# LayerNorm over partitions: variance and reciprocal root as whole-half tiles instead of compact token columns

## The chip, the cores and the metric

One core of one Trainium2 chip runs the kernel. The metric is the device time of one execution in microseconds (us): 6545.41 us is the median of three runs of the kernel before (6545.12 to 6548.72). Engines are called PE (TensorE matmul), PEld (TensorE's weight load), DVE (VectorE), ACT (ScalarE), POOL (GpSimd) and SP (the queue that issues the DMAs here).

## The reference, cut to what matters

The state x holds 16 batches of 56 tokens with 128 features each, all in fp32. Eight blocks follow one another, each adding its result to x: a six-layer diffusion transformer block with a context of 1500 tokens, a mixture of experts, a cross-attention block, an expert-choice layer, a latent cross-attention, a sparse mixer, slot attention and three fast-feed-forward trees. Every block starts from a LayerNorm of x, and the blocks have norms of their own. What matters is the norm:

```python
def _layernorm(x, axis=-1, eps=1e-05):
    m = jnp.mean(x, axis=axis, keepdims=True)
    v = jnp.var(x, axis=axis, keepdims=True)
    return (x - m) / jnp.sqrt(v + eps)

x = x + block(_layernorm(x, axis=-1), ...)     # eight times
```

In some uses the normed values are also scaled and shifted, by one factor per batch and feature (the adaptive norms of the cross-attention block) or one factor per feature.

## The kernel before, in words

x is kept in SBUF with the features on the 128 partitions and the 896 tokens (batch by batch) along the free axis. Most work is done by halves of 448 tokens, c = 0 and c = 1; `half(a, c)` is such a half. So a mean over features is a sum over partitions, and PE makes it: a matmul with `mean_w`, a 128x128 tile that holds 1/128 everywhere, leaves the mean of each token on all 128 partitions. An fp32 matmul shows as two MATMUL and two LDWEIGHTS records in the trace.

The program has one instruction stream per engine, written out by hand in `program`, block by block, and the engines meet only at semaphores. Twelve norms treat all 896 tokens at once through the helpers `ln_tensor`, `ln_scalar` and `ln_vector` (L253 to L303): the entry norm of each of the eight blocks (`LN_IN0`, `LN_MOE`, `LN_IN1`, `LN_EC`, `LN_IN2`, `LN_SM`, `LN_IN3`, `LN_FFF`), the three adaptive norms of the cross-attention block (`LN_L1(0)` to `LN_L1(2)`, with `per_batch`), and the norm of the latents (`LN_LAT`, with `per_feature`; `LN_IN3` also has `per_feature`). The norms inside the six layers of the first block (L1648, L1653, L1834 to L1839, L1987 to L1991) and those of the slot units (L3195 to L3200, L3264, L3371) have code of their own and are not touched. The first of these already takes its variance and its root over a whole half: L1653, L1991 (128x448), and the reciprocal L1839 over a quarter (128x224).

The steps of one such norm before the change, each done for c = 0 and then for c = 1:

1. PE L257: mean of the half, broadcast on all partitions, into PSUM bank c.
2. DVE L285: deviation = source minus mean.
3. ACT L274: square of the deviation into `ln_square`.
4. PE L261: four matmuls that use 112 tokens of the squares each as weights and one column of `mean_w` as the moving side; the variance of the 448 tokens comes out as a compact tile of 112 partitions by 4 columns in bank 2 + c. Both halves are 16 MATMUL records.
5. ACT L277: root of variance plus eps on the 112x4 tile, into `ln_token_stats`. Its function table is loaded ahead of it where ACT did something else before (ACT_TABLE_LOAD).
6. DVE L288: reciprocal of the 112x4 tile.
7. PE L266: four matmuls that spread the 112x4 tile to 128 partitions by 448 tokens, with a broadcast column as weights and the identity as the moving side, into bank 2 + c. Both halves are 16 MATMUL records.
8. DVE L292: deviation times the spread reciprocal root, read from PSUM, into the destination. With `per_batch` two more 128x448 operations per half follow (L297, L299), with `per_feature` one (L302); a drain stands ahead of each.

After the last half `ln_done` is signalled. PE waits for `ln_done(n, 1)`, the second half, at once behind `ln_tensor` (for instance L578, L730, L2575, L2580), except in the slot block, where a few small folding matmuls and one transposition of context tiles stand between the two (L3222 to L3225). After that wait come the router matmul L356 (expert blocks), the folding of weights L2367 (cross-attention block), the mean L257 of the following norm (`LN_LAT` behind `LN_IN2`) and the like. ACT and DVE go on in their own order: ACT to what the block does next, often with a table load, DVE to the block's own work, which mostly waits for PE.

Of the kernel before, what the change touches and what calls it, by code (L numbers as in the profile page):

```python
# [7 lines left out]
ALU, ACT, AX = mybir.AluOpType, mybir.ActivationFunctionType, mybir.AxisListType  # L8
# [4 lines left out]
HALF = T // 2  # L13
ROW, NQ = 112, 4
# [32 lines left out]
WHOLE = lambda n: n - 18 if n > LN_SLOT else n  # L47
N_WHOLE = WHOLE(N_LN)


class Signal:
# [3 lines left out]
    def __init__(self, sem, dims, step=1, base=0):  # L55
        self.sem, self.dims, self.step, self.base = sem, dims, step, base
# [44 lines left out]
def half(a, c):  # L101
    return a[:, c * HALF:(c + 1) * HALF]
# [6 lines left out]
def by_batch(a):  # L109
    return a.rearrange("p (b s) -> p b s", s=S)  # L110


def spread(cols, n):
    p, m = cols.shape
    return cols.unsqueeze(2).broadcast_to([p, m, n])


class Kernel:


    def __init__(self, nc, ctx, dr, out):
        self.nc, self.ctx, self.dr, self.out = nc, ctx, dr, out
        self.names, self.sems = {}, {}
        sb = lambda *a: self.sb(ctx, *a)
        self.x = sb("x_state", [128, T])[:, :]
        self.z = sb("block_state", [128, T])[:, :]
        self.xn = sb("x_normed", [128, T])[:, :]
        self.dev = sb("ln_deviation", [128, T])[:, :]
        self.sq = sb("ln_square", [128, T])[:, :]
        self.stats = sb("ln_token_stats", [ROW, 4, NQ])  # L130
        self.ident = sb("ident", [128, 128])
        self.ident_b = sb("ident_bf16", [128, 128], BF16)
        self.mean_w = sb("mean_weights", [128, 128])[:, :]
        self.gb = sb("adaln_scale_shift", [128, NORMS, 2, B])
        self.cond = sb("cond", [128, B])[:, :]
        self.c_mean = sb("context_mean", [KN, B, KT])
        self.c_rstd = sb("context_rstd", [KN, B, KT])
        self.eps_col = sb("eps", [128, 1])[:, :]
        self.psum = ctx.enter_context(nc.psum_tensor("psum", [128, 8, BANK], F32))
        self.consts_ready = self.events("consts_ready")  # L140
        self.in_arrived = self.events("in_arrived", step=32)
        self.ln_mean = self.events("ln_mean", N_LN, 2)
        self.ln_dev = self.events("ln_dev", N_LN, 2)
        self.ln_square = self.events("ln_square_ready", N_LN, 2)
        self.ln_var = self.events("ln_var", N_WHOLE, 2)
        self.ln_std = self.events("ln_std", N_WHOLE, 2)
        self.ln_rstd = self.events("ln_rstd", N_WHOLE, 2)
        self.ln_spread = self.events("ln_spread", N_WHOLE, 2)
        self.ln_done = self.events("ln_done", N_LN, 2)
        self.x_done = self.events("x_done", 8, 2)  # L150
        self.tokens_scored = self.events("tokens_scored", 4)
        self.rows_turned = self.events("rows_turned", 8, 2)
        self.rows_copied = self.events("rows_copied", 8, 2)
        self.gate_select = sb("gate_select", [128, 8], BF16)[:, :]
        self.gate_select32 = sb("gate_select_f32", [24, 8])[:, :]
        self.select_arrived = self.events("gate_select_arrived", step=16)
        self.select_ready = self.events("gate_select_ready")

    def sb(self, stack, name, shape, dt=F32):
        self.names[name] = self.names.get(name, 0) + 1  # L160
        if self.names[name] > 1:
            name = f"{name}_{self.names[name]}"
        return stack.enter_context(self.nc.sbuf_tensor(name, shape, dt))
# [89 lines left out]
def ln_tensor(e, k, n, src):  # L253


    for c in range(2):
        e.matmul(k.psum[:, c, 0:HALF], k.mean_w, half(src, c)).then_inc(k.ln_mean.sem, 1)  # L257
    for c in range(2):
        e.wait_ge(k.ln_square.sem, k.ln_square(n, c))
        for i in range(NQ):  # L260
            mm = e.matmul(k.psum[0:ROW, 2 + c, i:i + 1], half(k.sq, c)[:, i * ROW:(i + 1) * ROW], k.mean_w[:, 0:1])  # L261
        mm.then_inc(k.ln_var.sem, 1)
    for c in range(2):
        e.wait_ge(k.ln_rstd.sem, k.ln_rstd(WHOLE(n), c))
        for i in range(NQ):
            mm = e.matmul(k.psum[:, 2 + c, i * ROW:(i + 1) * ROW],  # L266
                          k.stats[:, 2 + c, i:i + 1].broadcast_to([ROW, 128]), k.ident[0:ROW, 0:ROW])
        mm.then_inc(k.ln_spread.sem, 1)


def ln_scalar(e, k, n):
    for c in range(2):
        e.wait_ge(k.ln_dev.sem, k.ln_dev(n, c))
        e.activation(half(k.sq, c), half(k.dev, c), ACT.Square).then_inc(k.ln_square.sem, 1)  # L274
    for c in range(2):
        e.wait_ge(k.ln_var.sem, k.ln_var(WHOLE(n), c))
        e.activation(k.stats[:, c, :], k.psum[0:ROW, 2 + c, 0:NQ], ACT.Sqrt, bias=k.eps_col[0:ROW, :]).then_inc(  # L277
            k.ln_std.sem, 1)


def ln_vector(e, k, n, src, dst, per_batch=None, per_feature=None):

    for c in range(2):
        e.wait_ge(k.ln_mean.sem, k.ln_mean(n, c))
        e.tensor_tensor(half(k.dev, c), half(src, c), k.psum[:, c, 0:HALF], ALU.subtract).then_inc(k.ln_dev.sem, 1)  # L285
    for c in range(2):
        e.wait_ge(k.ln_std.sem, k.ln_std(WHOLE(n), c))
        e.reciprocal(k.stats[:, 2 + c, :], k.stats[:, c, :]).then_inc(k.ln_rstd.sem, 1)  # L288
    for c in range(2):
        v = half(dst, c)  # L290
        e.wait_ge(k.ln_spread.sem, k.ln_spread(WHOLE(n), c))
        op = e.tensor_tensor(v, half(k.dev, c), k.psum[:, 2 + c, 0:HALF], ALU.mult)  # L292
        if per_batch is not None:
            v = by_batch(v)
            g, b = (spread(a[:, c * BH:(c + 1) * BH], S) for a in per_batch)
            e.drain()
            e.tensor_tensor(v, v, g, ALU.mult)  # L297
            e.drain()
            op = e.tensor_tensor(v, v, b, ALU.add)  # L299
        if per_feature is not None:  # L300
            e.drain()
            op = e.tensor_scalar(v, v, per_feature[0], per_feature[1], ALU.mult, ALU.add)  # L302
        op.then_inc(k.ln_done.sem, 1)  # L303
# [212 lines left out]
class GroupedExperts:  # L516
# [56 lines left out]
    def tensor(self, e):  # L573
        k = self.k
        e.wait_ge(k.x_done.sem, k.x_done(self.stage - 1, 1))
        ln_tensor(e, k, LN_MOE, k.x)
        e.wait_ge(self.router_arrived.sem, self.router_arrived())
        e.wait_ge(k.ln_done.sem, k.ln_done(LN_MOE, 1))  # L578
        tokens_tensor(e, k, 0, self.rw, self.E)
        e.wait_ge(self.chosen.sem, self.chosen())  # L580
        parts = self.parts[:, :, :, :].rearrange("p t j e -> p t (j e)")
        part_rows_tensor(e, k, 0, parts[:, :, 0:128], (0, 1), k.rows_turned)
        part_rows_tensor(e, k, 1, parts[:, :, 128:192], (2, 3), k.rows_turned)
        e.wait_ge(self.weights_arrived.sem, self.weights_arrived())
        e.wait_ge(k.rows_copied.sem, k.rows_copied(1, 1))
        e.wait_ge(self.cleared.sem, self.cleared())
        e.wait_ge(self.wide_ready.sem, self.wide_ready(1))
        self.experts.tensor(e)
# [90 lines left out]
class ExpertChoice:  # L679
# [67 lines left out]
    def scalar(self, e, ahead):  # L747
        ln_scalar(e, self.k, LN_EC)
        e.wait_ge(self.shifted.sem, self.shifted())
        e.activation(self.probs, self.probs, ACT.Exp).then_inc(self.exped.sem, 1)  # L750
        ahead.fold_scalar(e)
        self.experts.scalar(e)
# [51 lines left out]
class SparseMixer:  # L804
# [43 lines left out]
    def tensor(self, e):  # L848
        k = self.k
        e.wait_ge(k.x_done.sem, k.x_done(self.stage - 1, 1))  # L850
        ln_tensor(e, k, LN_SM, k.x)
        e.wait_ge(self.router_arrived.sem, self.router_arrived())
        e.wait_ge(k.ln_done.sem, k.ln_done(LN_SM, 1))
        tokens_tensor(e, k, 2, self.wg, self.E)
        e.wait_ge(self.gates_ready.sem, self.gates_ready())
        part_rows_tensor(e, k, 4, self.parts[:, :, :, :].rearrange("p t j e -> p t (j e)"), (0, 1), k.rows_turned)
        e.wait_ge(self.weights_arrived.sem, self.weights_arrived())
        e.wait_ge(k.rows_copied.sem, k.rows_copied(4, 1))
        e.wait_ge(k.select_ready.sem, k.select_ready())
        self.experts.tensor(e)  # L860
# [2788 lines left out]
```

## Time and profile before

| | us |
|---|---|
| median of the runs (lowest to highest) | 6545.41 (6545.12 to 6548.72) |
| the profiled execution's own time | 6548.03 |
| span of the profiled execution | 6546.2 |
| busy: PE, PEld | 6049.3, 4418.7 |
| busy: DVE, ACT, POOL | 3926.4, 3331.9, 2250.2 |

The span is the time between the first and the last record of the profile; the execution's own time is 1.8 us longer. Busy is the sum over an engine's instructions; the PE's matmul ends are modelled. The mean granted TensorE clock is 0.95 of full speed over the whole span; around the boundaries between blocks it is lower. The twelve norms lie at 35, 3468, 3635, 3660, 3828, 4668, 4703, 4817, 4824, 5824, 6000 and 6401 us from the start of the span.

### The profile page before, as it was taken

How to read it: one execution, taken by the hardware profiler on the slowest of the kernel's cores; microseconds unless marked ns; L12 is line 12 of the kernel's file. 1: busy time of each engine (PE TensorE's matmuls, PEld its weight loads, DVE VectorE, ACT ScalarE, POOL GpSimd, SP SyncE). 2: the span in 40 equal slices, each digit the busy share in tenths (PEclk: the TensorE clock that was granted, in tenths of full speed). 3: DMA queues.
4: the chain of work that ended last, by engine and by line, in shares of the span. 5: the costliest groups of instructions: out<-in, count | busy, mean ns of one | idle time of the engine just before them, and what ended most of it. 6: DMA issues, size and time to landing. Idle time of an engine off the chain costs nothing.

```text
span 6546.2 us, 141322 instructions
## 1 busy us (share of the span) xinstructions
PE 6049.3 (92%) x56229; PEld 4418.7 (68%) x56229; DVE 3926.4 (60%) x8713; ACT 3331.9 (51%) x6403; POOL 2250.2 (34%) x2198
## 2 busy tenths in 40 slices
PE   6899999999999999999997999999879999989997
PEld 4566666666666666666664777777657777765984
DVE  3776777777777777777775344444544444444553
ACT  1565656666566665666664334444333333333664
POOL 4555555555555555555540000000011111127440
PEclk7999999999999999999998899999889999998998
DMA  1665656656566665665661000000100000021000
GB/s 55 105 108 82 102 94 103 101 92 106 86 103 101 97 102 91 102 98 96 109 90 41 18 29 29 34 33 30 26 11 15 15 10 15 15 72 47 2 1 23
DMA packets 396488, 407.90 MB, mean 62 GB/s; under 512 B 125575, under 2 KB 372946, under 8 KB 393786
## 3 DMA queue, kind: packets, MB, share of 16 engines
q1 hardware_dynamic: 395834, 398.85, 34.3%
q8 instruction: 450, 7.37, 0.6%
q14 instruction: 204, 1.67, 0.1%
HBM read 158.00 MB, written 0.46 MB: 24 GB/s over the span
## 4 chain that ended last, share of the span: by engine, by line
PE 69%; DVE 8%; POOL 7%; issue 6%; ACT 4%; DMA 2%; SPq 1%; POOLq 1%; DVEq 0%; ACTq 0%
PE psum L2244 10%; PE psum L2211 9%; PE psum L1581 6%; PE psum L1569 6%; PE psum L1555 6%; PE psum L1595 4%; PE psum L2256 4%; PE psum L1603 4%; PE psum L1701 3%; POOL slot_context L3444 2%; DVE row_max L1920 2%; PE psum L421 2%; PE psum L435 2%; PE psum L1710 1%; DMA key_stack<-key_parts 1%
## 5 line engine op out<-in xcount | busy, mean ns | idle before, releaser
L1920 DVE TENSOR_REDUCE row_max<-psum 112x1 f32<-112x500 f32 x2304 | 1443.3, 669 | 283.3 <-PE psum L1569 278.6
L2041 ACT ACTIVATE weights<-psum 125x448 f32<-125x448 f32 x2304 | 1155.3, 544 | 771.7 <-PE psum L1555 757.1
L1555 PEld LDWEIGHTS psum<-query_stack,key_stack 121*125 121x125 bf16 x9216 | 830.8, 140 | 369.5 <-issue 166.9
L1569 PE MATMUL psum<-key_stack,query_stack 97*112 97x500 bf16 x2304 | 904.8, 393 | 105.6 <-DVE row_max L1920 78.9
L1555 PE MATMUL psum<-query_stack,key_stack 121*125 121x112 bf16 x9216 | 932.7, 224 | 70.2 <-ACT weights L2041 65.0
L2244 PE MATMUL psum<-l_ctx_v,l_turned 125*128 125x128 f32 x5376 | 713.6, 281 | 16.1 <-ACT l_turned L2282 12.0
L2324 DVE TENSOR_REDUCE l_stat<-psum 128x1 f32<-128x1500 f32 (+1 forms) x224 | 391.7, 1749 | 542.3 <-PE psum L2211 542.3
L2244 PEld LDWEIGHTS psum<-l_ctx_v,l_turned 125*128 125x128 f32 x5376 | 643.1, 191 | 58.9 <-ACT l_turned L2282 40.0
L1581 PE MATMUL psum<-weights,values 125*17 125x112 f32 x18432 | 678.7, 266 | 0.2 <-ACT weights L2041 0.2
L1581 PEld LDWEIGHTS psum<-weights,values 125*17 125x17 f32 x18432 | 379.7, 98 | 264.1 <-ACT weights L2041 144.1
L2061 POOL TENSOR_TENSOR key_temp<-key_temp,rope_sin 128x500 f32<-128x500 f32 x288 | 359.5, 1248 | 502.2 <-DVE key_temp L1805 502.2
L2071 POOL TENSOR_TENSOR key_parts<-key_temp,key_parts 128x500 bf16<-128x500 f32 x288 | 327.1, 1136 | 545.1 <-ACT key_parts L1950 545.1
L2282 ACT ACTIVATE l_turned<-psum 125x512 f32<-125x512 f32 x448 | 251.3, 597 | 431.9 <-PE psum L2256 429.2
L2068 POOL TENSOR_TENSOR key_temp<-key_temp,key_parts 128x500 f32<-128x500 f32 x288 | 327.1, 1136 | 363.9 <-ACT key_parts L1946 363.9
L2256 PE MATMUL psum<-ident,l_weights 128*125 128x128 f32 (+1 forms) x2800 | 400.3, 276 | 19.4 <-ACT l_keys L2791 8.0
L2941 POOL MEMSET l_turned<- 125x128 f32 x2 | 0.4, 218 | 1179.5 <-DVE x_state L801 1179.5
L2256 PEld LDWEIGHTS psum<-ident,l_weights 128*125 128x125 f32 (+1 forms) x2800 | 348.3, 184 | 82.5 <-issue 38.9
L1569 PEld LDWEIGHTS psum<-key_stack,query_stack 97*112 97x112 bf16 x2304 | 307.7, 134 | 140.5 <-issue 74.2
L2065 POOL TENSOR_TENSOR key_temp<-key_temp 128x500 f32<-128x500 f32 x288 | 358.0, 1243 | 41.9 <-POOL key_temp L2061 0.9
L2307 ACT ACTIVATE l_weights<-psum,l_stat 128x1500 f32<-128x1500 f32 (+1 forms) x224 | 344.1, 1536 | 35.9 <-DVE l_stat L2324 35.9
L1595 PE MATMUL psum<-ctx_t,l_w_context 128*128 128x500 f32 x576 | 340.2, 674 | 2.1 <-ACT values L1967 2.1
L1603 PE MATMUL psum<-l_w_context,ctx_t 128*125 128x128 f32 x2304 | 339.9, 292 | 0.0
(539 smaller groups left out, 10276.6 us busy)
## 6 DMA issues: line engine op xcount, KB each, us to landing
key_stack<-key_parts SPq DMA_DIRECT2D x1728, 125.0 KB, 4.4
ctx_t<-in_ctxT SPq DMA_DIRECT2D x96, 750.0 KB
l_ctx_v<-in_ctxV SPq DMA_DIRECT2D x32, 750.0 KB
query_stack<-query_parts SPq DMA_DIRECT2D x576, 28.0 KB, 3.7
l_ctx_t<-in_ctxT SPq DMA_DIRECT2D x16, 750.0 KB
slot_context<-in_ctxV SPq DMA_DIRECT2D x16, 750.0 KB
key_stack<-ctx_mask_rows SPq DMA_DIRECT2D x576, 3.9 KB
sm_w<-in_sm_w SPq DMA_DIRECT2D x3, 2048.0 KB
```

Source lines behind the costliest of these rows:

```text
L1555: mm = e.matmul(self.k.psum[0:KN, h, (p % 4) * QC:(p % 4 + 1) * QC], ks[:, p, kt * KN:(kt + 1) * KN], q[:, p * QC:(p + 1) * QC])
L1569: e.matmul(self.k.psum[0:QC, 2 + n % 2, 0:500], q[0:ROWS_MAX, p * QC:(p + 1) * QC], ks[0:ROWS_MAX, p, c * 500:(c + 1) * 500]).then_inc(sel ...
L1581: mm = e.matmul(self.k.psum[32 * j:32 * j + 17, 5, g * QC:(g + 1) * QC], v[:, kt, p, :], w[:, p * QC:(p + 1) * QC], start=kt == 0 and g == ...
L1595: e.matmul(side.bank(*key)[:, 0:500], self.wk[b // B % 2][:, 0, :], self.ctx_t[b % 2][:, c * 500:(c + 1) * 500]).then_inc(side.filled, 1)
L1603: mm = e.matmul(side.bank(*key)[0:KN, i * 128:(i + 1) * 128], self.ctx_t[b % 2][:, t * KN:(t + 1) * KN], self.wk[b // B % 2][:, 1, :])
L1920: e.tensor_reduce(self.largest[:, i % PAIRS, i // PAIRS:i // PAIRS + 1], k.psum[0:QC, 2 + i % 2, 0:500], AX.X, ALU.max, negate=True).then_ ...
L2041: e.activation(half(self.p[kt % 2], h), self.k.psum[0:KN, h, 0:HALF], ACT.Exp).then_inc(self.exped.sem, 1)
L2061: e.tensor_tensor(tm[:, 1, :], tm[:, 1, :], self.sin[:, c * 500:(c + 1) * 500], ALU.mult).then_inc(self.key_turned_sin.sem, 1)
L2211: mm = e.matmul(k.psum[:, c, 0:self.step], q[:, r * 128:(r + 1) * 128], self.keys(b)[:, c * self.step:(c + 1) * self.step])
L2244: mm = e.matmul(k.psum[:, 6, 0:128], pt[:, t, :], v[:, t, :], start=t == 0, stop=t == self.tiles - 1)
L2256: tr = e.transpose(bk[0:rows, t * 128:(t + 1) * 128], self.p[j % 2][:, c0:c0 + rows], k.ident[:, :])
L2324: e.tensor_reduce(self.stat[i % 4][:, 1:2], k.psum[:, 0:self.n_s, 0:self.step], AX.XY, ALU.max, negate=True).then_inc(self.max_ready.sem, 1)
```

## The change

The compact tile and its spreading go. The variance becomes one matmul per half of `mean_w` with the half of the squares, and comes out broadcast on 128 partitions (L261 and L266 become this one). The root reads that PSUM bank, 128x448, and writes it over the squares. The reciprocal works in place on these 128x448 elements in SBUF. The product takes both operands from SBUF. Per half, DVE now does reciprocal, product and what follows before it turns to the other half; before, both reciprocals came ahead of both products. The semaphore `ln_spread` and the tile `ln_token_stats` are dropped, and DVE waits for its own reciprocal through `ln_rstd`.

```diff
@@ ln_tensor @@
         e.matmul(k.psum[:, c, 0:HALF], k.mean_w, half(src, c)).then_inc(k.ln_mean.sem, 1)
     for c in range(2):
         e.wait_ge(k.ln_square.sem, k.ln_square(n, c))
-        for i in range(NQ):
-            mm = e.matmul(k.psum[0:ROW, 2 + c, i:i + 1], half(k.sq, c)[:, i * ROW:(i + 1) * ROW], k.mean_w[:, 0:1])
-        mm.then_inc(k.ln_var.sem, 1)
-    for c in range(2):
-        e.wait_ge(k.ln_rstd.sem, k.ln_rstd(WHOLE(n), c))
-        for i in range(NQ):
-            mm = e.matmul(k.psum[:, 2 + c, i * ROW:(i + 1) * ROW],
-                          k.stats[:, 2 + c, i:i + 1].broadcast_to([ROW, 128]), k.ident[0:ROW, 0:ROW])
-        mm.then_inc(k.ln_spread.sem, 1)
+        e.matmul(k.psum[:, 2 + c, 0:HALF], k.mean_w, half(k.sq, c)).then_inc(k.ln_var.sem, 1)
@@ ln_scalar @@
     for c in range(2):
         e.wait_ge(k.ln_var.sem, k.ln_var(WHOLE(n), c))
-        e.activation(k.stats[:, c, :], k.psum[0:ROW, 2 + c, 0:NQ], ACT.Sqrt, bias=k.eps_col[0:ROW, :]).then_inc(
-            k.ln_std.sem, 1)
+        e.activation(half(k.sq, c), k.psum[:, 2 + c, 0:HALF], ACT.Sqrt, bias=k.eps_col).then_inc(k.ln_std.sem, 1)
@@ ln_vector @@
     for c in range(2):
+        v, inv = half(dst, c), half(k.sq, c)
         e.wait_ge(k.ln_std.sem, k.ln_std(WHOLE(n), c))
-        e.reciprocal(k.stats[:, 2 + c, :], k.stats[:, c, :]).then_inc(k.ln_rstd.sem, 1)
-    for c in range(2):
-        v = half(dst, c)
-        e.wait_ge(k.ln_spread.sem, k.ln_spread(WHOLE(n), c))
-        op = e.tensor_tensor(v, half(k.dev, c), k.psum[:, 2 + c, 0:HALF], ALU.mult)
+        e.reciprocal(inv, inv).then_inc(k.ln_rstd.sem, 1)
+        e.wait_ge(k.ln_rstd.sem, k.ln_rstd(WHOLE(n), c))
+        op = e.tensor_tensor(v, half(k.dev, c), inv, ALU.mult)
         if per_batch is not None:
```

## Rows read from the trace of the kernel before

**Rows 1.** The page: lines of the chain that ended last, shares of the span

```profile
PE psum L2244 10%; PE psum L2211 9%; PE psum L1581 6%; PE psum L1569 6%; PE psum L1555 6%; PE psum L1595 4%; PE psum L2256 4%; PE psum L1603 4%; PE psum L1701 3%; POOL slot_context L3444 2%; DVE row_max L1920 2%; PE psum L421 2%; PE psum L435 2%; PE psum L1710 1%; DMA key_stack<-key_parts 1%
```

**Rows 2.** Chain of waits through LN_MOE: start us, us, what

```profile
3473.01 1.28 ACT L277
...
3474.84 3.26 PE psum L266 x16
...
3478.12 0.63 DVE x_normed L292
...
3478.89 3.24 PE psum L356 x14
```

**Rows 3.** L266 alone by stretch: PE busy, PEld busy, granted clock, DMA share, GB/s

```profile
4816.00:4825.00 9.00, 2.04 (x16) 1.86 (x16) 1.00 0.20 41
3635.00:3645.00 10.00, 3.75 (x16) 3.48 (x16) 0.71 0.23 79
```

**Rows 4.** Groups by line and shape, reciprocals: xcount | busy us, mean ns | idle before

```profile
L1839 DVE RECIPROCAL ln_deviation<-ln_deviation 128x224 f32<-128x224 f32 x72 | 111.0, 1544 | 12.4 <-ACT ln_deviation L1991 9.7
...
L3345 DVE RECIPROCAL slot_stat<-slot_stat 125x12 f32<-125x12 f32 x48 | 10.9, 228 | 3.5
...
L2713 DVE RECIPROCAL context_rstd<-context_rstd 125x192 f32<-125x192 f32 x1 | 1.4, 1353 | 0.6 <-ACT context_rstd L2670 0.6
```

**Rows 5.** A root (as rows 4); a product (source line: min/median/max ns)

```profile
L1991 ACT ACTIVATE ln_deviation<-psum,eps 128x448 f32<-128x448 f32 x36 | 22.8, 634 | 7.4 <-PE psum L1653 7.1
...
L3375 DVE TENSOR_TENSOR slot_normed<-slot_deviation,psum x36: 374/384/390, 6015.7 to 6399.3; 128x224 f32<-128x224 f32 x36
```

**Rows 6.** Timeline of LN_IN1: start us, us, engine, line, operation, idle before

```profile
3639.39 0.42 ACT L277 ACTIVATE ln_token_stats<-psum,eps 112x4 f32<-112x4 f32 x2
...
3643.70 0.62 DVE L292 TENSOR_TENSOR block_state<-ln_deviation,psum 128x448 f32<-128x448 f32 x1 [1.08 <-PE psum L266]
```

**Rows 7.** Timeline of LN_IN2 and of LN_SM's router matmul

```profile
4821.10 0.42 ACT L277 ACTIVATE ln_token_stats<-psum,eps 112x4 f32<-112x4 f32 x2
...
4823.70 0.62 DVE L292 TENSOR_TENSOR x_normed<-ln_deviation,psum 128x448 f32<-128x448 f32 x1 [0.27 <-PE psum L266]
...
5831.22 1.70 PE L356 MATMUL psum<-sm_gate_w,x_normed 128*128 128x8 f32 x14 [0.81 <-DVE x_normed L292]
```

**Rows 8.** Timeline of LN_L1(1), per batch

```profile
3833.65 0.26 ACT L277 ACTIVATE ln_token_stats<-psum,eps 112x4 f32<-112x4 f32 x1
...
3838.88 0.63 DVE L297 TENSOR_TENSOR x_normed<-x_normed,adaln_scale_shift 128x448 f32<-128x448 f32 x1
3839.58 0.62 DVE L299 TENSOR_TENSOR x_normed<-x_normed,adaln_scale_shift 128x448 f32<-128x448 f32 x1
```

**Rows 9.** Timeline of LN_LAT, per feature

```profile
4824.38 1.77 PE L257 MATMUL psum<-x_normed,mean_weights 128*128 128x448 f32 x4 [0.71 <-DVE x_normed L292]
...
4825.44 1.37 DVE L285 TENSOR_TENSOR ln_deviation<-x_normed,psum 128x448 f32<-128x448 f32 x2 [1.11 <-PE psum L257]
...
4826.72 1.73 PE L261 MATMUL psum<-mean_weights,ln_square 128*112 128x1 f32 x16 [0.57 <-ACT ln_square L274]
...
4831.30 0.51 DVE L302 TENSOR_SCALAR x_normed<-x_normed,l_affine 128x448 f32<-128x448 f32 x1
```

**Rows 10.** Timeline of LN_IN3, per feature, and POOL beside it

```profile
5995.35 17.27 POOL L3444 TENSOR_SCALAR slot_context<-slot_context,context_mean,context_rstd 125x128 f32<-125x128 f32 x22
...
6004.59 0.42 ACT L277 ACTIVATE ln_token_stats<-psum,eps 112x4 f32<-112x4 f32 x2
...
6009.61 0.54 DVE L302 TENSOR_SCALAR block_state<-block_state,slot_sigma,slot_cols 128x448 f32<-128x448 f32 x1
```

**Rows 11.** Timeline of LN_FFF

```profile
6400.75 3.35 PE L257 MATMUL psum<-x_state,mean_weights 128*128 128x448 f32 x4 [1.51 <-DVE x_state L3392]
...
6405.28 0.25 ACT L277 ACTIVATE ln_token_stats<-psum,eps 112x4 f32<-112x4 f32 x1
...
6408.87 0.62 DVE L292 TENSOR_TENSOR x_normed<-ln_deviation,psum 128x448 f32<-128x448 f32 x1 [0.86 <-PE psum L266]
```

More of the change, by code:

```diff
@@ L129, in __init__ @@
         self.sq = sb("ln_square", [128, T])[:, :]
-        self.stats = sb("ln_token_stats", [ROW, 4, NQ])
         self.ident = sb("ident", [128, 128])
@@ L147, in __init__ @@
         self.ln_rstd = self.events("ln_rstd", N_WHOLE, 2)
-        self.ln_spread = self.events("ln_spread", N_WHOLE, 2)
         self.ln_done = self.events("ln_done", N_LN, 2)
```

## The prediction

> **What bounds the kernel now.** I read the page first. PE is busy for most of the span, so the first question is whether the change touches time in which PE works, or time in which PE stands and others work for it. The lines that carry the chain of waits are attention matmuls; none of the changed lines is among the large ones [rows 1]. What the change touches are twelve short stretches between blocks in which PE, ACT and DVE work for each other by turns. So I read the chain of waits through one such stretch, LN_MOE [rows 2]: table load, (root, reciprocal,) sixteen records of the spreading matmul, the second product, then the router matmul. Every piece starts when the one before it ends, and no DMA is in it. An engine's share of busy time says nothing here; what is added between the square and the last product is added to the end. Third I read timelines of the norms for two times each, the start of the first root and the end of the last DVE instruction; what stands between them is what the change replaces.
>
> **What it removes.** The spreading matmuls L266: 3.26 us of the chain in LN_MOE, 3.75 us in LN_IN1, where the granted clock was 0.71 on average, 2.04 us in LN_IN2, where it was 1.00 [rows 2, 3]. The 112x4 root, 0.25 us [rows 11], and the 112x4 reciprocal, which is no dearer than the 12-element one (0.23 us [rows 4]). The small variance matmuls, 1.73 us for both halves [rows 9], for which four records of a broadcast matmul come, of the kind of L257: 1.77 us at the full clock [rows 9], 3.35 us in the slow state of the clock [rows 11].
>
> **The variance matmul.** Where ACT loads the root's table ahead of the first root (eight norms), the matmul of the first half ends under that load: in LN_MOE the load ends at 3473.01 + 1.28 = 3474.29 [rows 2]. So these norms' first root starts when it does now, and I cost the matmul at nothing; its cover is the 1.28 us load, and without it the price is that of the next case. In LN_LAT, LN_FFF and two of the adaptive norms the table is loaded already. In LN_LAT the first mean takes from 4824.38 to the start of the deviation at 4825.44, 1.06 us [rows 9]; a variance begun at 4826.72 is therefore there at 4827.77, against 4827.71 for the small ones, almost no loss.
>
> **The root.** The same operation over 128x448 from PSUM is in the trace: 0.634 us [rows 5]. The second root runs under the first reciprocal.
>
> **The reciprocal** is the term that decides. No row shows it over 448 elements. The rows give 0.228 us for 12 elements a partition, 1.353 us for 192 and 1.544 us for 224 [rows 4]; 224 less 12 elements are 1.316 us, 6.2 ns an element. The number of partitions doesn't matter to it, the number of elements does, and a whole half has 112 times the 4 of before. 448 elements are then 1.544 + 224 x 6.2 ns = 2.93 us. The bounds: by the last two rows alone 6.0 ns an element, 2.88 us; twice 1.544 us is 3.09 us. I take 2.93. It is six times the cost of the product of the same size (0.62 us [rows 6]).
>
> The Trainium skill (VectorE: DVE Perf Modes, the walkthrough of the 8-slice pipeline) says that the reciprocal is an iterated divide with a repeat count of 8 in the same pipe. The trace agrees that it is no streaming operation, but the row has less than eight steps of a product's pace; by the rule the price would be higher (third rival).
>
> **The product** now reads both operands from SBUF. The same form is there as L297 with 0.63 us, against 0.62 us for L292 [rows 8]: no difference.
>
> **The new path of a plain norm** from the first root's start: root 0.63, handover 0.04, then on DVE, one after the other, 2 x (2.93 + 0.07 + 0.62), with 0.07 for the wait on its own semaphore as between L297 and L299 (start to start 0.70 [rows 8]). Sum 7.91 us. It is DVE's alone; the clock of PE no longer matters to it. Per batch four more instructions at 0.70: 10.71. Per feature two more at about 0.60: 9.11. Before, the first half's extra instructions ran while PE spread the second half; that cover is gone, which is why norms with extra steps lose more.
>
> Against the trace:
> - LN_IN1: 3639.39 + 7.91 = 3647.30, before 3644.32 [rows 6]: +2.98. LN_IN0 and LN_EC have the same pattern to 0.02 us: three times, +8.9.
> - LN_MOE: 3474.29 + 7.91 against 3478.75 [rows 2]: +3.5.
> - LN_FFF: 6405.30 + 7.91 against 6409.49 [rows 11]: +3.7.
> - LN_IN2: 4821.10 + 7.91 against 4824.32 [rows 7]: +4.7; LN_SM has the same pattern. These two spread at the full clock and lose more. +9.4.
> - LN_L1(1): 3833.65 + 10.71 against 3840.20 [rows 8]: +4.2; the other two adaptive norms by the same sum +4.7 and +4.4. +13.2.
> - LN_LAT: 4827.77 + 9.11 against 4831.81 [rows 9]: +5.1.
> - LN_IN3: 6004.59 + 9.11 against 6010.15 [rows 10]: +3.6.
>
> Sum +47.4 us.
>
> **What else moves.** PE now stands for about 8 us in each norm instead of working on L266 in between. Where the next PE work ran at the full clock, it may start at the low level: LN_SM's router matmul (fourteen records) took 1.70 us, LN_MOE's 3.24 us [rows 2, 7], a possible +1.5. LN_LAT's mean and variance behind LN_IN2 at the low level: half of 3.35 - 1.77 [rows 9, 11] twice, +1.6. I take both, +3. In the other norms the work behind is at the low level already. ACT's following table loads stay hidden under the reciprocals. No DMA is added or moved. SP's queue waits for a norm in the first block only (the loads behind `ln_done(LN_IN0, 1)`), and shifts with it. POOL has nothing in the changed helpers. What is queued behind DVE's longer occupation is the block's own work, which needs the normed tokens anyway.
>
> Total +50 us on the profiled execution: span 6596, its own time 6598. That execution was 2.6 us above the median of the runs shown; on the median I get 6595 us, slower by 0.77%. What a measurement of this kernel can tell from no change is about 0.2%, 13 us.
>
> **The rivals.**
>
> First, *the reciprocal streams* (the side of not slower). If a wide reciprocal in place cost what the product costs, 0.62 us, twenty-four of them would be 55 us cheaper than I say, and the time would be 6545 + 50 - 55 = 6540 us. The place is DVE's chain in each norm; the point where it decides is a price of 2.93 - 50/24 = 0.85 us, below which the change is no loss. For it: nothing was measured at 448. Against: 72 instances of half the size at 1.54 us, in the same in-place fp32 form, and one of 192 elements while POOL was idle [rows 4]. 2%.
>
> Second, *cover at the slots*. POOL's scaling of the context, L3444, is a line of the chain [rows 1], and it runs until 6012.6, past the end of LN_IN3 at 6010.15 [rows 10]. If the slots' start hangs on POOL and not on the queries, the losses of LN_SM and LN_IN3 (4.7 + 3.6 us, and 1.5 of the clock) vanish: 6585 us. Against: what POOL does behind it waits for the first attention weights, which need the normed slots. 6%.
>
> Third, *eight full steps an element*. From 224 to 448 elements a product goes from 0.384 to 0.62 us, 1.05 ns an element [rows 5, 6]; eight of these are 8.4 ns, a reciprocal of 3.8 us, and 24 x 0.87 = +21: 6616 us. Against: the slope of 6.2 ns. This is the page's rule named above. 2%.
>
> Fourth, *the clock gives back*. Broadcast matmuls of 448 columns keep the array busier than one-column ones; if the granted clock then stayed full into the next work, nine norms would each save about the 1.5 us of a router matmul, and the +3 would not come: 6595 - 17 = 6578 us. Against: PE stands for 8 us behind them. 5%.
>
> Fifth, the change *doesn't do what it says*: if the second half waited for something else, or the code were unchanged in effect, 6545 us. The diff leaves no room for it. 1%.
>
> **How the numbers follow.** The forecast has 84%. Its own spread: the reciprocal's bounds are -1 and +4 us; whether each following stage wakes at the low or full clock is worth up to 1.5 us in each of twelve places, say -6 to +8. That is 6585 to 6606; the second rival adds little below, so the range is 6583 to 6607. Slower by over 0.2% holds in all cases but the first, the fifth and half a per cent of coincidence: slower 0.96, within 0.2% 0.03, faster 0.01.
>
> **What would show it.** In the profile after: L288's successor with 24 instances of 128x448 at 2.9 us each, some 70 us of DVE busy time more; the root at 0.63 us; in each norm the two products 3.6 us apart; in the chain of waits two reciprocals in each norm in place of L266; the stretch from first root to last DVE instruction 7.9, 9.1 and 10.7 us for the three kinds; block boundaries shifted step by step by 3 to 5 us, and nothing between them changed. I am wrong if the reciprocal's mean is not 2.9 us, or if a shift at a norm is not found again at the next block's end.

## The result, and the profile after

The changed kernel takes 6606.3 us in the median of four runs (6601.7 to 6608.7), the kernel before 6547.1 us (6545.1 to 6553.2). The ratio is 1.0088 with a 95% interval of 1.0071 to 1.0105: slower by 58 us, between 46 and 69. The profiled execution has a span of 6604.0 us and a mean granted clock of 0.948, against 6546.2 and 0.95.

The page after, busy times (before: PE 6049.3, DVE 3926.4, ACT 3331.9):

```profile
PE 6028.3 (91%) x55893; PEld 4380.2 (66%) x55893; DVE 3991.9 (60%) x8713; ACT 3339.0 (51%) x6403; POOL 2247.3 (34%) x2198
```

DVE has the same number of instructions and 65 us more to do; PE has 336 records and 21 us less. The groups by line and shape show where (columns: count | busy us, mean ns | idle before):

```profile
L278 DVE RECIPROCAL ln_square<-ln_square 128x448 f32<-128x448 f32 x24 | 70.8, 2949 | 27.7 <-ACT ln_square L267 27.7
L258 PE MATMUL psum<-ln_square,mean_weights 128*128 128x448 f32 x48 | 27.1, 685 | 6.3 <-ACT ln_square L264 6.1
```

The reciprocal over a half, the term that no row of before showed, takes 2.949 us; the forecast from [rows 4] was 2.93. The chain of waits through LN_MOE, which answers to [rows 2]:

```profile
3488.46 1.28 ACT L267
...
3489.76 0.64 ACT ln_square L267
...
3490.42 2.96 DVE ln_square L278
...
3493.41 0.62 DVE x_normed L280
3494.03 2.87 DVE ln_square L278
...
3496.93 0.64 DVE x_normed L280
3497.56 0.14 issue
3497.70 3.24 PE psum L344 x14
```

Read it from above: where sixteen records of the spreading matmul stood, there are now two reciprocals with a product behind each, all on DVE. From the first root's start to the end of the last product it is 7.81 us, against 7.91 in the forecast (the second reciprocal starts under the tail of the first product, which I had left out).

To see where the 58 us arise, I cut every profile at the twelve norms: a norm is the time from the start of its first mean matmul to the end of its last DVE instruction, a stretch the time from there to the next norm. These are read from timeline rows; the columns are the norms in their order, without the LN_ of their names, and the last lines are later profiles of the same two programs.

| us | IN0 | MOE | IN1 | L1(0) | L1(1) | L1(2) | EC | IN2 | LAT | SM | IN3 | FFF | sum |
|---|---|---|---|---|---|---|---|---|---|---|---|---|---|
| before | 11.3 | 10.3 | 9.3 | 10.4 | 12.5 | 10.8 | 9.3 | 7.6 | 7.4 | 7.6 | 9.8 | 8.7 | 114.9 |
| after | 14.3 | 12.2 | 12.2 | 15.7 | 16.5 | 15.0 | 12.7 | 12.1 | 14.0 | 12.2 | 14.4 | 12.3 | 163.4 |
| before, second | 10.9 | 7.8 | 7.6 | 10.4 | 12.5 | 10.8 | 9.3 | 7.6 | 7.4 | 7.6 | 9.8 | 8.8 | 110.4 |
| before, third | 11.3 | 7.8 | 7.6 | 10.5 | 12.5 | 10.7 | 9.3 | 7.6 | 7.4 | 7.6 | 9.8 | 8.7 | 110.7 |
| after, second | 14.2 | 12.2 | 12.2 | 15.7 | 16.5 | 15.0 | 12.7 | 12.2 | 13.9 | 12.2 | 14.5 | 12.3 | 163.3 |

The norms alone give +48.5 us between the two first profiles. The rest, +9.3 us, lies between norms, and nearly all of it in one stretch: the six layers of the first block, from the end of LN_IN0 to the start of LN_MOE, took 3422.1 us before and 3435.7 us after. The other stretches changed by -3.2 (block behind LN_LAT), +3.0 (behind LN_SM), -3.3 (behind LN_IN3), -0.9 (behind LN_MOE) and not more than 0.4 us each.

### The profile page after: what moved, and what is told of

Same layout as the page of the kernel before. It is cut to its first block, busy times and chain, and to the rows that moved or that the text cites. A ratio compares the mean times of both kernels' runs of the same rounds, so it can differ in the third digit from the quotient of the medians.

```text
span 6604.0 us, 140650 instructions
## 1 busy us (share of the span) xinstructions
PE 6028.3 (91%) x55893; PEld 4380.2 (66%) x55893; DVE 3991.9 (60%) x8713; ACT 3339.0 (51%) x6403; POOL 2247.3 (34%) x2198
## 4 chain that ended last, share of the span: by engine, by line
PE 68%; DVE 9%; POOL 7%; issue 6%; ACT 4%; DMA 2%; SPq 1%; POOLq 1%; DVEq 0%; ACTq 0%
PE psum L2232 10%; PE psum L2199 9%; PE psum L1569 6%; PE psum L1557 6%; PE psum L1543 6%; PE psum L2244 4%; PE psum L1583 4%; PE psum L1591 3%; PE psum L1689 3%; POOL slot_context L3432 2%; DVE row_max L1908 2%; PE psum L409 2%; PE psum L423 2%; PE psum L1698 1%; DMA key_stack<-key_parts 1%
## 5 line engine op out<-in xcount | busy, mean ns | idle before, releaser
L2232 PE MATMUL psum<-l_ctx_v,l_turned 125*128 125x128 f32 x5376 | 713.7, 281 | 16.0 <-ACT l_turned L2270 12.1
```

The costliest lines, as they stand in the source:

```text
L2232: mm = e.matmul(k.psum[:, 6, 0:128], pt[:, t, :], v[:, t, :], start=t == 0, stop=t == self.tiles - 1)
```

## The experiments

Theory A: the layers of the first block run longer because their start is shifted, so the change costs some 13 us there. Theory B: they vary from execution to execution, and the change costs what the norms cost. Beside that stood the question whether the reciprocal is all of the loss, and what PE's standing does.

### The first norm alone, and the eleven others

Both kernels keep the two forms of the helpers side by side and choose by the norm:

```diff
+NEW = (LN_IN0,)      # in the other kernel all norms but LN_IN0
+def ln_vector(e, k, n, *a, **kw):
+    (ln_vector_whole if n in NEW else ln_vector_compact)(e, k, n, *a, **kw)
...
```

> The new form in the first norm of the program (LN_IN0) alone, the compact form in the other eleven. Theory A (the layers of the first block run about 13 us longer because their start is shifted by the norm's 3 us): about 6547 + 3 + 13 = 6563 us, and the stretch from the end of LN_IN0 to the start of LN_MOE 13 us longer than the 3422 us of before. Theory B (those 13 us were a matter of the single execution, the layers are of varying length from run to run): about 6550 us in the median, and a stretch that may lie anywhere in a band of some 15 us. The norm itself by both: +3.0 us.

> The new form in eleven norms, LN_IN0 as before. The norms' own losses in the profile of the changed kernel sum to 48.5 us, 3.0 of them in LN_IN0. Theory A: 6547 + 45.5 = 6592 us, stretch of the first block's layers as before. Theory B: 6592 us plus whatever the layers add in these executions, no relation to LN_IN0; if the sum of both partial kernels' losses is that of the whole change, no interaction is left.

Measured: LN_IN0 alone 6559.5 us (11 runs) against 6547.9 (21 runs), ratio 1.0013 with an interval of 1.0001 to 1.0026, which is 1 to 17 us. All but LN_IN0 6598.5 us, ratio 1.0074 (1.0054 to 1.0095), 35 to 62 us. The medians don't part the theories: 3 us and 16 us both lie in the first interval. The layers' stretch was 3440.0 us in the profile of the first and 3437.7 us in that of the second. The second speaks against theory A: its LN_IN0 is as before, and its layers were 16 us longer than in the first profile all the same. The two losses, 8.5 and 48.5 us by their ratios, add up to 57, that of the whole change. An interaction doesn't show, but with these two intervals one of 10 us wouldn't either.

The profile of the first kernel shows one thing more. Its eleven other norms have the compact form, instruction for instruction as before, and yet they sum to 106.3 us, against 103.6, 99.5 and 99.5 in the three profiles of before. LN_LAT took 11.2 us in it instead of 7.4, LN_IN3 11.2 instead of 9.8, and the router matmul behind LN_SM 3.13 us instead of 1.70. LN_LAT's mean reads there:

```profile
4838.19 3.35 PE L259 MATMUL psum<-x_normed,mean_weights 128*128 128x448 f32 x4 [0.71 <-DVE x_normed L323]
```

It took 1.77 us in every profile of before, behind the same wait of 0.71 us [rows 9]. So the level of the clock at these late boundaries differs from execution to execution by itself, or shifts with something far ahead; one profile can't tell which. Some 3 to 7 us of that execution come from norms whose form was not changed.

### The same programs again

Both programs unchanged, for further profiles.

> The kernel before once more, for a second profile. Theory B (the layers of the first block differ from execution to execution whatever the norms are): the stretch from the end of LN_IN0 to the start of LN_MOE, 3422.1 us in the first profile, lies anywhere between 3420 and 3440. Theory A (the shifted start makes them longer): 3422 to within 3 us. All other stretches between norms as in the first profile, to 3 us.

> The changed kernel once more, for a second profile. Theory B: the stretch of the first block's layers, 3435.7 us in the first profile, lies anywhere between 3420 and 3440; theory A: 3436 to within 3 us. The sum of the twelve norms is 163 us again to within 3, since their length hangs on DVE and the table load and little on the clock.

Measured: the layers' stretch took 3427.1 us in the second profile of before and 3419.6 us in the second of after, shorter than any of before. That execution took 6589.1 us instead of 6606, 17 us less, and 16 of them are this stretch. With all kernels of this study the stretch lies between 3420 and 3441 us. Theory B holds for the 13 us of the first pair of profiles. A mean effect of a few us isn't excluded: four profiles with the old LN_IN0 at its old place give 3429 us in the mean, six with the new one 3433, with single values up to 14 us away from these. That stays open.

A third profile of before:

> The kernel before for a third profile. LN_MOE took 10.27 us in the first and 7.84 in the second, LN_IN1 9.29 and 7.58, all others the same to 0.4 us. If that is the clock's level at the end of the first block, which differs from execution to execution with the length of its layers, this profile has LN_MOE at one of the two values or between and all others as before; the layers' stretch again between 3419 and 3440 us.

It has LN_MOE at 7.76 and LN_IN1 at 7.57 us, layers at 3429.2. So two of three executions of before have these two norms 2.5 and 1.7 us shorter than the one on which I made the sum. The timeline of the second profile shows why: the spreading matmul of LN_MOE took 2.29 us there, and its mean matmul ran at the full clock, 1.77 us for four records instead of 3.25:

```profile
3473.71 1.77 PE L257 MATMUL psum<-x_state,mean_weights 128*128 128x448 f32 x4 [1.97 <-DVE x_state L1925]
...
3478.59 2.29 PE L266 MATMUL psum<-ident,ln_token_stats 112*128 112x112 f32 x16 [0.74 <-DVE ln_token_stats L288]
```

In the first profile of before the same line reads:

```profile
3468.47 3.25 PE L257 MATMUL psum<-x_state,mean_weights 128*128 128x448 f32 x4 [1.97 <-DVE x_state L1925]
```

The stretch behind LN_IN1 goes with it: 16.0 us in the first profile of before and in all of the changed kernel, 13.5 and 13.4 in the other two of before. The new form doesn't have this variation between root and product, since no matmul lies there (7.8 us in all plain norms of every profile); between mean and root it still has it.

### The reciprocal's price taken away

```diff
-        e.reciprocal(inv, inv).then_inc(k.ln_rstd.sem, 1)
+        e.tensor_scalar(inv, inv, 0.0, 0.05, ALU.mult, ALU.add).then_inc(k.ln_rstd.sem, 1)
```

The stand-in writes a constant, so the division by the root is left out.

> In the reciprocal's place stands a one-source DVE instruction of the same 128x448 tile in place that writes a constant (so the normed values are not the reference's: the division by the root is left out). It shows what the change is worth without the price of the reciprocal. My theory (the reciprocal of 2.95 us is the whole loss): each of the 24 becomes about 0.5 us, 24 x 2.44 = 58.6 us less than the changed kernel, about 6548 us, and the stretch from first root to last DVE instruction of a plain norm 2.9 us against 7.8. Rival (the loss is PE's idle time and the clock, or the wide root): the time stays above 6580 us.

Measured: 6543.9 us (11 runs), ratio to before 0.9988 (0.9976 to 1.0000), 62 us below the changed kernel. The stand-in's source line (min/median/max ns), and LN_IN2 in the timeline:

```profile
L278 DVE TENSOR_SCALAR ln_square<-ln_square x24: 384/394/1317, 42.3 to 6396.7; 128x448 f32<-128x448 f32 x24
```

```profile
4812.14 1.16 ACT L267 ACTIVATE ln_square<-psum,eps 128x448 f32<-128x448 f32 x2
...
4814.19 0.63 DVE L280 TENSOR_TENSOR x_normed<-ln_deviation,ln_square 128x448 f32<-128x448 f32 x1
```

24 x (2.949 - 0.394) = 61.3 us by the stand-in's median; the sum of the norms fell from 163.4 to 100.9, by 62.5. The stretch from root to the last product is 2.68 us in LN_IN2. So the rest of the change (broadcast variance, wide root, no spreading) is a gain against before in the norms: 100.9 against 110.4 to 114.9 us. In the medians (3 us less, an interval up to 1.0000) this gain is hardly to be told. The reciprocal is the whole loss and more.

### PE kept at work

```diff
+    for _ in range(10):
+        e.matmul(k.psum[:, 0, 0:128], k.mean_w, k.mean_w)
```

> The changed kernel with ten 128x128 fp32 matmuls of the mean weights with themselves behind the variance matmuls of every norm, into a PSUM bank that nobody reads then, so that PE doesn't stand during the reciprocals. If the clock theory holds (LN_LAT's extra 1.7 us and the slower router matmul of LN_SM come from PE having stood for 8 us), LN_LAT's mean and variance and LN_SM's router matmul run at the full level again and the time falls by 3 to 8 us, to about 6600. If PE's activity doesn't matter, 6606 and the same rows as in the changed kernel.

Measured: 6600.8 us, ratio 1.0082 (1.0059 to 1.0104), the changed kernel within error. But LN_LAT's mean still took 3.36 us and LN_SM's router matmul 3.12: the expectation missed, because the filler was too short. The ten products took 2.4 us of the 8 us wait and PE stood for 5.9 us more. So a second kernel filled the wait, in two norms only:

```diff
+    for _ in range(30 if n in (LN_IN2, LN_SM) else 0):
+        e.matmul(k.psum[:, 0, 0:128], k.mean_w, k.mean_w)
```

> The changed kernel with thirty 128x128 fp32 matmuls of the mean weights behind the variance matmuls of LN_IN2 and LN_SM alone: by the rows of the kernel with ten (2.39 us) they last 7.2 us and fill PE's wait of 8.1 us nearly to its end. If the clock falls because PE stands, LN_LAT's mean takes 1.77 us again instead of 3.35 and LN_SM's router matmul 1.70 instead of 3.12, and LN_LAT is 1.7 us shorter (12.3 instead of 14.0): 3 us in all, not to be told from noise in the median. If they still take 3.35 and 3.12, the level comes from something else.

The timeline of this kernel behind LN_IN2, and LN_SM's router matmul:

```profile
4851.30 6.86 PE L260 MATMUL psum<-mean_weights 128*128 128x128 f32 x60
...
4859.56 1.77 PE L255 MATMUL psum<-x_normed,mean_weights 128*128 128x448 f32 x4 [1.40 <-DVE x_normed L282]
...
5876.15 1.70 PE L346 MATMUL psum<-sm_gate_w,x_normed 128*128 128x8 f32 x14 [1.49 <-DVE x_normed L282]
```

The changed kernel has in the same places:

```profile
4866.43 3.35 PE L255 MATMUL psum<-x_normed,mean_weights 128*128 128x448 f32 x4 [8.09 <-DVE x_normed L280]
...
5881.22 3.12 PE L344 MATMUL psum<-sm_gate_w,x_normed 128*128 128x8 f32 x14 [8.19 <-DVE x_normed L280]
```

Look at the last column: PE stood 1.4 us before the mean instead of 8.1, and the same four records take half the time. LN_LAT is 12.4 us instead of 14.0. This mean took 3.35 or 3.36 us in all five profiles of the new form in which PE had stood for 5.9 to 8.1 us ahead of it (the kernels after, after again, all but LN_IN0, ten products, and the changed kernel with the preload below), and 1.77 us here and in the kernel with the stand-in, where PE had stood for 3.0 us. So a long wait of PE brought the low level every time, and filling it brought the full one. It is not the only way to the low level: in the kernel with LN_IN0 alone PE stood for 0.71 us and the mean took 3.35 us all the same, as shown above. LN_SM's router matmul goes the same way in each of them, at 3.12 or 1.70 us. Apart from the two programs themselves, each kernel has one profile.

The median is 6604.8 us (ratio 1.0087, 1.0074 to 1.0101), no gain that can be told. In this profile the stretch behind LN_LAT, which had been 3.2 us shorter in the changed kernel than before (988.5 against 991.7 us), is 991.9 us again. That looks as if the clock gave back in the next stretch what it took at the boundary, but other profiles speak against it: the kernel with the stand-in has LN_LAT at the full level (7.3 us) and 988.6 us behind it, the changed kernel with the preload has it at the low level (14.1 us) and 991.9 us. What moves this stretch by 3 us stays open.

### The table load

Two kernels load the root's table before the norm needs it, one on the kernel before and one on the changed kernel:

```diff
 def ln_scalar(e, k, n):
+    e.activation(k.root_table, k.eps_col, ACT.Sqrt)      # 128x1, ahead of the first wait
     for c in range(2):
```

> The kernel before with one root of a single column (eps) at the head of ln_scalar, ahead of its first wait, so that the root's table is loaded while ACT waits for the deviation. Eight norms have the load between square and root now. If the load is on the path where the chain shows it, the first root starts about 1 us earlier in these eight, the spreading matmuls with it: 6 to 10 us less in all, about 6540 us. If it were hidden by the variance matmuls of the second half, no difference in the norms' sum of 115 us.

> The changed kernel with the root's table loaded ahead, as in the kernel preload. In eight norms the load of 1.28 us stands between square and root; without it the first root waits for the variance matmul of the first half, there about 1.0 us earlier. The chain of DVE behind it is unchanged (7.8, 9.0, 10.6 us). So the sum of the twelve norms falls from 163 to about 155 us, the median to about 6598 us, still 0.8% above the kernel before: the table load and the reciprocals are separate terms. Rival: the reciprocals hide the load, nothing changes.

Measured: on the kernel before 6541.0 us (12 runs) against 6551.1 (17 runs), ratio 0.9984 with an interval of 0.9975 to 0.9993: 5 to 16 us faster. It beats both kernels. The norms' sum is 103.1 us, against 110.4 to 114.9. LN_L1(0) and LN_FFF, where no load stood, are 1.8 us longer in it, with more of their small matmuls at the low level. The load in its timeline ahead of LN_IN2, beside PE's last matmuls of the block before:

```profile
4788.61 4.67 PE L437 MATMUL psum<-hidden,ec_down 128*128 128x448 f32 x12
...
4790.24 1.28 ACT L273 ACT_TABLE_LOAD   x1
...
4797.86 0.27 ACT L279 ACTIVATE ln_token_stats<-psum,eps 112x4 f32<-112x4 f32 x1 [0.28 <-PE psum L262]
```

The root now waits for PE (L262), not for the load. On the changed kernel the preload gives a sum of norms of 155.0 us, as forecast, and 6595.2 us (ratio 1.0069, 1.0052 to 1.0086; without the preload 1.0088, 1.0071 to 1.0105, so in the medians this gain is not clear of noise). The two terms are separate: against the second profile of before, from the first mean matmul to the first root it is 1.0 us less in LN_MOE, LN_IN1, LN_EC, LN_IN2 and LN_SM of the compact form, 1.8 in LN_IN0, 1.4 in LN_L1(1) and nothing in LN_IN3, whose mean ran at the low level in that profile; in the wide form, against the changed kernel, it is 0.6 to 1.5 us less in each of the eight. No preload saves the form with the wide reciprocal.

## Why the prediction was right

The forecast was 6595 us, 0.77% slower, in a range of 6583 to 6607; the median is 6606.3, 0.88% slower. It is at the edge of the range, and that it lies inside is in part luck: the interval of 46 to 69 us reaches beyond the upper end, which stands for 60 us, and the first block's layers, of which the forecast says nothing, move by more than the 0.7 us that was left. The mechanism and the deciding term are shown. Step by step:

- **The reciprocal**, the deciding term: 2.93 us from a slope of 6.2 ns an element, measured 2.949. (That this is "six times" the product of the same size was a slip: 2.93 by 0.62 is 4.7; six is the ratio of the slopes, 6.2 to 1.05 ns an element.) The streaming rival (6540 us) and the rival of eight full steps (3.8 us each, 6616 us) are out by the row L278. The run with the stand-in shows what the streaming rival's world would be: 6543.9 us.
- **The path of a plain norm**: 7.91 us from root to last product, measured 7.78 to 7.81; per batch 10.71, measured 10.6; per feature 9.11, measured 8.97. All a little high by the same 0.1 us, the overlap left out.
- **The root** 0.63 us for the first, measured 0.64, the second under the reciprocal; **the product** from SBUF 0.62 us, unchanged.
- **The variance matmul at no cost**: right under the table load (first root unchanged to 0.01 us in LN_IN1, LN_L1(1), LN_IN2, LN_SM). In LN_L1(0), where no load covers it, the root came 0.7 us later at the low clock, in LN_IN0 0.2 and in LN_L1(2) 0.1: about 1 us that I had at nothing. In LN_EC and LN_IN3 the root came 0.5 and 1.1 us later as well, but not for the variance: the mean matmul, which the change doesn't touch, ran at the low clock and held up the second square and the table load behind it. LN_IN3 before and after:

```profile
6000.33 1.67 PE L257 MATMUL psum<-x_state,mean_weights 128*128 128x448 f32 x4
...
6003.29 1.28 ACT L277 ACT_TABLE_LOAD   x1
```

```profile
6053.34 2.81 PE L255 MATMUL psum<-x_state,mean_weights 128*128 128x448 f32 x4
...
6057.43 1.28 ACT L267 ACT_TABLE_LOAD   x1
```

From the mean's start to the load's it is 2.96 us before and 4.09 after. The kernel with LN_IN0 alone, compact in LN_IN3, has 4.49 us there.
- **Standing PE and the clock**: +1.6 us in LN_LAT, measured 1.7 us later root; +1.5 in LN_SM's router matmul, measured +1.4. The kernel that filled the wait takes both away; that the same two losses also appeared in one execution without a long wait makes them a matter of the execution as well. The stretches behind them changed too, which I had not foreseen (-3.2, +3.0, -3.3 us): "nothing between them changed", one of the signs that the prediction named, did not hold to better than 3 us.
- **What was mis-sized**: the sum "against the trace". It set the new path, which hardly varies, against one execution of before in which LN_MOE and LN_IN1 ran in part at the low clock: 10.3 and 9.3 us. In the two other profiles of before they took 7.8 and 7.6. The loss there is 4.3 and 4.6 us instead of the 3.5 and 3.0 that I summed, and the norms' whole loss is 163.4 - 110.5 = 53 us, where I had 49 with LN_LAT's clock term. Without the first block's layers the stretches between the norms add up to 1 us less than in the second profile of before. I had said how the execution's total stood to the median, but not asked whether its norms were typical.
- **The range** doesn't come out of its own terms: 6595 us with -1 and +4 for the reciprocal and -6 and +8 for the clock gives 6588 to 6607, not 6585 to 6606. It changes nothing at the upper end, where the result lies.
- **The rest to 58 us** is not to be told: over all kernels here the layers of the first block move by 21 us (by 7 in three profiles of before, by 16 in two of the changed kernel), and the interval is 46 to 69.
- **Cover at the slots** (second rival): the norms there are longer by 4.5 us, and POOL's scaling ends at 6057.9 us, 10 us before LN_IN3 does. The stretch behind LN_IN3 is 3.3 us shorter; but it was about as short (387.9 us) in the kernel with only LN_IN0 changed, so nothing speaks for a cover. **The clock gives back** (fourth rival, 6578 us): the one-sided gain it needed didn't appear. **The change** did what it says: 24 wide reciprocals and no spreading matmul stand in the trace.

## What to carry to other kernels

A statistic of a token belongs in a compact tile for as long as an expensive operation works on it. Broadcasting first saves a matmul of 2 to 4 us, but it multiplied the elements of the reciprocal by 112, and on this engine a reciprocal costs 6 ns an element where a product costs 1: price every operation at its new width before moving the broadcast ahead of it. Where an activation table is switched inside a short dependent chain, ask for it with a one-column dummy before the wait that starts the chain; that was worth 5 to 16 us here. And before summing against one profile, look at a second: the clock's level at a boundary moved single norms by 2.5 us between profiles of one program, and by 3.8 us between two programs that are the same in that norm.

## What I had not expected of the hardware

The Trainium skill (ScalarE: Activation LUTs, What ACT_TABLE_LOAD costs) gives about 1283 ns for the load and about 1380 ns for a drain, 2.66 us together for a switch to a different set. The load agrees: every load of the root's table in these traces takes 1.283 us. The drain doesn't show: in LN_MOE before the change the load begins 0.01 us after the last square and the root 0.02 us after the load (3473.01 + 1.28, then 3474.31), so the switch cost 1.3 us in all, and the measurement decides. The filler of thirty small matmuls in a wait of 8 us kept the granted clock at its full level for the matmul behind it (1.77 us), while one that ended 5.9 us before it did not (3.36 us).

The executions of one and the same program differ by more than I took for granted: 6537 to 6575 us over 21 runs of the kernel before. The two profiles of the changed kernel, 17 us apart, have 16 us of that in the first block's layers, where DMA, POOL and PE hand keys to each other; which of these hand-overs varies was not tried. The three profiles of before lie within 2 us of each other and can't place its spread.
